# Pointwise steps and sums over K on 32x32 pieces of the array, the second sums moved ahead of V's step, VectorE's order changed, the first copy of Q moved

## The chip, the core and the metric

The kernel runs on one core of one Trainium2 chip. The metric is device time in microseconds (us), the median of several executions. TensorE (PE; its weight loads are PEld) multiplies, VectorE (DVE) and ScalarE (ACT) work on tiles, GpSimd (POOL) does small powers and gathers rows, and SyncE (SP) issues most transfers. Each engine has its own instruction queue and they meet at semaphores.

## What is computed

One layer over 6250 tokens of 256 channels: graph attention, a linear attention in hyperbolic form, and a feed-forward part with a router that picks 2 of 8 experts. The change touches the linear attention alone. Cut to that (the sequence has length one here, so each convolution is a product or a scale):

```python
h = conv1d(logmap0(proj(x)), w_qkv)             # 256 -> 768 channels
t = relu(batchnorm(h))                          # then expmap0, proj, logmap0
s = conv1d(t, w_dw, groups=768)                 # a scale per channel
s = conv1d(s, w_pw, groups=24)                  # 24 blocks of 32x32
q, k, v = split(concat([t, s]))                 # 16 groups of 3 * 32 channels
q, k = relu(q), relu(k)
vk = einsum('ngdl,ngel->ngde', v, k)            # l = 1: v times the sum over k
out = einsum('ngde,ngdl->ngdl', vk, q)
out = out / (sum(v, -1) + 1e-15)
ft = conv1d(out, w_res) + b_res                 # 512 -> 256 channels
```

With one position per sequence, `out` is q times the sum over a group's 32 values of k, where v is not zero. A group of 32 channels takes 32 partitions, so both the pointwise step `w_pw` and the sum over k (a product with a block matrix of ones, `bo`) are 32x32 blocks along the diagonal.

## The kernel before

Tokens lie in 25 blocks (`NB`) of 250 (`BT`), each block of two tiles (`TB`) of 125. Channels lie on partitions, in six chunks of 128: Q in chunks 0 and 1, K in 2 and 3, V in 4 and 5. "T" is the half of the attention that works on `t`, "S" the half that works on the pointwise result `s`.

The program has three stretches. Up to about 204 us the input is scaled and turned, the graph tables are written, and the 256 to 768 product (L1215) is made for all blocks with its batch statistics. From about 204 to 450 us a loop runs over the blocks; the change is there. After that come the router and the two experts.

The loop is one list of steps for each engine, written out by hand, each step with its lag in blocks: in step s a stage with lag 2 works on block s - 2. `steps(NB, [...])` runs each list. Each engine goes through its list strictly in order, and a stage begins with the waits that it needs.

- TensorE: `pointwise_kq` (lag 0; the pointwise step of Q and K), `turn_norms` (1), `res` (2; the product with `w_res`, L1335), `pointwise_v` (0; the pointwise step of V, and with it the sums over K for T), `k_sums_s` (0; the sums over K for S), `turn_xn` (4; L1349), `norms` (0; sums of squares, L1313 and L1316). In the first step `k_sums_s` stands ahead of `pointwise_v`.
- ScalarE: `tanh` (3), `square_s` of K, `keep_k`, `square_s` of Q, `keep_q` (all 0), the ReLU of V of the next block (L931), `square_o` (1; L998), `square_s` of V (0; L959), `square_u` (2; L1007), `more_relu` (steps 1 to 4 only: five blocks' Q), `keep_xn` (4; L1032), `keep_norms` (0; L1027), `square_t` of the next block (L983).
- VectorE: `make_x1` (3), `check_t` (0), `divide_where_needed` (1), statistics of x1 (3), `make_u` (2; L1976 and L1983), `attend_s` (0; L1901), `check_s` (0), `attend_t` (0; L1893 and L1896), `make_xn` (3), `keep_turned` (0), a piece of the graph part (`late_now`).

`divide_where_needed` reads a flag. Where it is set, a long branch divides by sum(v) + 1e-15; otherwise the branch is jumped. In both cases it then raises `fixed`, for which `pointwise_v` of the next block waits. The branch is taken once in this run.

## Time and profile before

| | us |
|---|---|
| median of 3 runs | 791.08 |
| lowest, highest | 790.62, 791.55 |
| profiled execution | 792.75 |
| span of its instructions | 790.7 |
| TensorE busy | 744.1 (94%) |
| VectorE busy | 590.1 (75%) |
| ScalarE busy | 500.8 (63%) |
| GpSimd busy | 509.9 (64%) |

A busy engine is one with an instruction in work; matmuls overlap, and their ends are modelled. The profiled execution is 1.67 us over the median, and 2.05 us of it lie outside the span.

### The profile page before, as it was taken

Reading aid. Unit: us, or ns where it says so; the run is one execution under the profiler, and the core shown is the slowest. Engines: PE = TensorE matmul, PEld = TensorE weight load, DVE = VectorE, ACT = ScalarE, POOL = GpSimd, SP = SyncE. Lnnn points to the kernel's source line nnn.
Section 4 is the critical chain, followed back from the end, with each engine's and each line's share of the span. In section 5 each row is a group of like instructions: output and inputs, shape, how many; then the busy total and the mean of one; then the engine's idle time right before and its main releaser. Section 6 shows DMA issues by size and latency. Waiting matters only on the chain.

```text
span 790.7 us, 16845 instructions
## 1 busy us (share of the span) xinstructions
PE 744.1 (94%) x5512; PEld 624.8 (79%) x5512; DVE 590.1 (75%) x1693; ACT 500.8 (63%) x1163; POOL 509.9 (64%) x693
## 2 busy tenths in 40 slices
PE   5899999999899999999929989999999999999995
PEld 4678888888666666666626677999999999999994
DVE  6873478888769898888997865766776777677675
ACT  2567344989889888888828616555555555555640
POOL 3430678777457888888826742576677766768654
PEclk9999999999999999999968999999999999999999
DMA  9855122222102211111110113000000000000001
GB/s 213 219 155 159 44 54 53 61 49 60 30 19 63 61 54 45 52 35 55 32 43 25 38 33 102 4 24 28 14 27 23 18 27 21 21 27 15 27 27 40
DMA packets 35430, 41.43 MB, mean 52 GB/s; under 512 B 11520, under 2 KB 20696, under 8 KB 35339
## 3 DMA queue, kind: packets, MB, share of 16 engines
q1 hardware_dynamic: 22355, 30.71, 13.4%
q0 software_dynamic: 8000, 6.82, 4.0%
q10 hardware_dynamic: 4984, 2.79, 1.5%
q8 instruction: 45, 0.74, 0.4%
q14 instruction: 46, 0.38, 0.2%
HBM read 25.59 MB, written 14.60 MB: 51 GB/s over the span
## 4 chain that ended last, share of the span: by engine, by line
PE 74%; DVE 6%; POOL 6%; issue 5%; ACT 5%; DMA 2%; SPq 0%; POOLq 0%; DVEq 0%; ACTq 0%
PE ps L1465 18%; PE ps L1504 17%; PE ps L1335 10%; PE ps L1225 7%; PE ps L1215 6%; PE ps L1313 5%; PE ps L1194 4%; ACT Z L931 3%; POOL asrc L622 2%; PE ps L1519 2%; PE ps L1349 2%; PE ps L1323 2%; POOL L L619 1%; ACT Z L927 1%; PE ps L1182 1%
## 5 line engine op out<-in xcount | busy, mean ns | idle before, releaser
L1215 PE MATMUL ps<-Z,L 128*128 128x250 f32 x600 | 126.9, 373 | 0.0
L1215 PEld LDWEIGHTS ps<-Z,L 128*128 128x128 f32 x600 | 113.6, 189 | 13.2
L1086 ACT ACTIVATE Z<-Z,b1s 128x250 f32<-128x250 f32 x144 | 70.0, 503 | 71.7 <-DVE Z L2147 71.7
L1335 PE MATMUL ps<-wr,Z 128*125 128x256 f32 x400 | 92.7, 384 | 0.0
L931 ACT ACTIVATE Z<-Z,bn_o,bn_s 128x250 f32<-128x250 f32 x150 | 81.2, 598 | 1.0 <-DVE bn_o L1855 1.0
L1093 ACT ACTIVATE L<-ps 128x250 f32<-128x250 f32 x144 | 54.3, 379 | 42.9 <-PE ps L1465 40.8
L1335 PEld LDWEIGHTS ps<-wr,Z 128*125 128x125 f32 x400 | 73.1, 188 | 10.2 <-issue 0.4
L2147 DVE TENSOR_TENSOR Z<-ps,L 128x250 f32<-128x250 f32 x144 | 59.4, 415 | 19.5 <-PE ps L1465 17.2
L1225 PE MATMUL ps<-Z,pw 64*64 64x250 f32 x600 | 55.5, 389 | 16.8 <-issue 15.1
L619 POOL DMA_INDIRECT L<-xt_table,idst x36 | 44.2, 1228 | 40.5 <-issue 39.3
L1736 DVE BATCH_NORM_STATS2 L<-Z 128x6 f32<-128x250 f32 x140 | 49.2, 407 | 26.3 <-ACT Z L927 26.2
L927 ACT ACTIVATE Z<-ps 128x500 f32<-128x500 f32 x75 | 43.4, 579 | 30.9 <-PE ps L1215 29.5
L771 POOL TENSOR_TENSOR L<-Z 128x500 f32<-128x500 f32 x23 | 31.5, 1368 | 46.0 <-ACT Z L1086 46.0
L622 POOL DMA_INDIRECT asrc<-xt_table,isrc x40 | 48.6, 1215 | 12.2 <-issue 12.2
L1465 PE MATMUL ps<-Z 128*128 128x250 f32 x192 | 56.3, 374 | 0.0
L1225 PEld LDWEIGHTS ps<-Z,pw 64*64 64x64 f32 x600 | 26.2, 134 | 37.8 <-issue 25.1
L1194 PE MATMUL ps<-L,Z 128*125 128x264 f32 x200 | 50.5, 398 | 0.9 <-ACT Z L883 0.9
L1313 PE MATMUL ps<-L,ones 128*32 128x250 f32 x600 | 49.0, 387 | 1.1 <-issue 0.8
L1504 PEld LDWEIGHTS ps<-Z 128*125 128x125 f32 x368 | 47.2, 187 | 2.0
L1504 PEld LDWEIGHTS ps<-L 128*125 128x125 f32 x368 | 47.1, 187 | 2.0
L1504 PE MATMUL ps<-Z 128*125 128x128 f32 x368 | 47.7, 272 | 0.0
L1504 PE MATMUL ps<-L 128*125 128x128 f32 x368 | 47.5, 272 | 0.0
(274 smaller groups left out, 2000.0 us busy)
## 6 DMA issues: line engine op xcount, KB each, us to landing
Z<-in_x SPq DMA_DIRECT2D x25, 250.0 KB
out<-L SPq DMA_DIRECT2D x24, 250.0 KB
xt_table<-L SPq DMA_DIRECT2D x25, 231.0 KB
Z<-in_x SPq DMA_DIRECT2D x1, 2016.0 KB
g_table<-gg SPq DMA_DIRECT2D x25, 62.5 KB
gg<-g_table SPq DMA_DIRECT2D x25, 62.5 KB
Z<-in_x SPq DMA_DIRECT2D x1, 1344.0 KB
Z<-in_w SPq DMA_DIRECT2D x2, 512.0 KB, 3.7
```

Source lines behind the costliest of these rows:

```text
L622: g.indirect_dma_start(left_at[:, t, :], None, xt_table, bass.IndirectOffsetOnAxis(ap=isrc[0:TP, j:j + 1].bitcast(U32), axis=0), element_o ...
L931: a_.activation(zc(b, c), zc(b, c), ACT.Relu, bias=bn_o[:, c:c + 1], scale=bn_s[:, c:c + 1]).then_inc(done.sem, 1)
L1086: a_.activation(to, of, ACT.Gelu, bias=b1s[:, f // NF, f % NF:f % NF + 1]).then_inc(gelu_done, 1)
L1093: a_.activation(kp[:, s, k - 1], ps[:, bank, 0:BT], ACT.Copy).then_inc(product_kept[s].sem, 1)
L1194: last = mm(ps[0:TP, 2 + 2 * (b % 2) + t, 0:XT], h_raw(b, k)[:, t * TP:(t + 1) * TP], wg[:, k, :], start=(k == 0), stop=(k == KD - 1))
L1215: last = mm(ps[:, group_bank(n), h * BT:(h + 1) * BT], wq[:, k, c * 128:(c + 1) * 128], h_raw(b, k), start=(k == 0), stop=(k == KD - 1))
L1225: return mm(to[cols_], lhsT[rows_, HALF * a:HALF * a + HALF], rhs[rows_], start=True, stop=True)
L1313: last = mm(ps[32 * q:32 * q + 32, 5, 0:BT], ones[:, 0:32], of, start=(i == 0), stop=(i == 3), skip_group_check=True)
L1335: last = mm(res_bank(b, t), ob(b, c, 1)[:, t * TP:(t + 1) * TP], wr[:, c, :], start=(c == 0), stop=(c == NO - 1))
L1465: mm(ps[:, bank, 0:BT], of, by, start=first, stop=True, skip_group_check=True).then_inc(product[s].sem, 1)
L1504: last = mm(ps[0:TP, bank, 0:HD2], of[:, k], by[:, k], start=(first and k == 0), stop=(k == NF - 1), skip_group_check=True)
L2147: v_.tensor_tensor(to, ps[:, bank, 0:BT], kp[:, s, k - 1], ALU.add).then_inc(product_sum[s].sem, 1)
```

## The change

`quarter` becomes `group`: a product of 32 rows by 32 columns of the array, with row piece i going to column piece i XOR step. The steps are chosen so that the sixteen products of Q and K, and the sixteen of V and the T sums, all use different 32x32 pieces; the eight S sums use eight different ones. Each stage has twice as many matmuls. Results of four row pieces that share a column piece go to four banks, so the banks are laid out anew, and `turn_xn` now uses bank 2, which is also K's first bank. K's channels, their weights and parameters are reordered to match (`K_TURN`), `w_res`'s last chunk is loaded in two halves, and the long branch loses two copies because V's result already lies where it is needed. Core of the diff:

```diff
+        K_TURN = (1, 3)
+        Q_STEP, K_STEP, V_STEP, KST_STEP, KSS_STEP = (0, 2), (1, 3), (0, 2), (1, 3), (0, 2)
+        Q_BANK, K_BANK, SUM_BANK, NORM_BANK, V_BANK, RES_BANK = 0, 2, 3, 4, 5, 7
+        XN_BANK = K_BANK
+        KSS_AT = 260
...
             square_s(0, R_Q)
+            keep_q(0)
             act.wait_ge(bn_done.sem, bn_done.count(2))
...
-                (0, keep_q),
+                (0, later(keep_q)),
...
-            def quarter(to, lhsT, rhs, a, e):
-
-                rows_, cols_ = slice(HALF * a, HALF * a + HALF), slice(HALF * e, HALF * e + HALF)
-                return mm(to[cols_], lhsT[rows_, HALF * a:HALF * a + HALF], rhs[rows_], start=True, stop=True)
+            def group(to, lhsT, rhs, i, step):
+
+                rows_, cols_ = slice(GROUP * i, GROUP * i + GROUP), slice(GROUP * (i ^ step), GROUP * (i ^ step) + GROUP)
+                return mm(to[cols_], lhsT[rows_, GROUP * i:GROUP * i + GROUP], rhs[rows_], start=True, stop=True)
...
-                    pe.wait_ge(att.sem, att.count(b - 1, 1))
+                    pe.wait_ge(att.sem, att.count(b - 1, 2))
+                    if b >= 5:
+                        pe.wait_ge(xn_kept.sem, xn_kept.count(b - 5))
...
-                for h in range(NH):
-                    cq, ck = 2 * R_Q + h, 2 * R_K + h
-                    for a in range(2):
-                        quarter(bank_half(R_Q, h), pw[:, cq, :], zc(b, cq), a, a)
-                        last = quarter(bank_half(R_K, h), pw[:, ck, :], zc(b, ck), a, 1 - a)
+                for i in range(4):
+                    for h in range(NH):
+                        cq, ck = 2 * R_Q + h, 2 * R_K + h
+                        group(bank_half(Q_BANK + h, 0), pw[:, cq, :], zc(b, cq), i, Q_STEP[h])
+                        last = group(bank_half(K_BANK + h, 0), pw[:, ck, :], zc(b, ck), i, K_STEP[h])
...
+                pe.wait_ge(s_sq.sem, s_sq.count(b, 2))
+                pe.wait_ge(k_kept.sem, k_kept.count(b))
+                pe.wait_ge(q_kept.sem, q_kept.count(b))
+                for i in range(4):
+                    for h in range(NH):
+                        cv, ck = 2 * R_V + h, 2 * R_K + h
+                        last_v = group(bank_half(V_BANK + h, 1), pw[:, cv, :], zc(b, cv), i, V_STEP[h])
+                        last_k = group(bank_half(Q_BANK + h, 1), bo, zc(b, ck), i, KST_STEP[h])
...
-                    pe.wait_ge(att.sem, att.count(b - 1))
+                    pe.wait_ge(att.sem, att.count(b - 1, 1))
+                    pe.wait_ge(nrm_kept.sem, nrm_kept.count(b - 1))
...
                     pe.wait_ge(s_sq.sem, s_sq.count(b))
+                    pe.wait_ge(att.sem, att.count(b, 1))
...
-                (0, lambda b: None if b else k_sums_s(b)),
+                (0, k_sums_s),
                 (0, pointwise_v),
-                (0, lambda b: k_sums_s(b) if b else None),
...
             def attend_s(b):
                 dve.wait_ge(q_kept.sem, q_kept.count(b))
+                dve.wait_ge(kst_done.sem, kst_done.count(b))
+                dve.wait_ge(t_sq.sem, t_sq.count(b))
                 dve.wait_ge(kss_done.sem, kss_done.count(b))
```

The two waits on `att` are those of `pointwise_kq` and `k_sums_s`; the third, added one is in `norms`. VectorE's list now begins with `check_t`, then `make_x1`, and has `attend_s`, `make_u`, `attend_t`, `check_s` where it had `make_u`, `attend_s`, `check_s`, `attend_t`. On ScalarE the copies of K's weights (R_K of `wq`) are six instead of four, twice, and `w_res` is loaded by three transfers instead of one. The tail's idle matmuls and the first hidden products change banks.

How this stands on TensorE, one step of the loop from the sixth on, before (L1225 are the quarters, L1323 `turn_norms`, L1335 `res`, L1349 `turn_xn`, L1313 `norms`):

```order
L1225 MATMUL ps<-Z,pw 64x250 [waits q_kept,k_kept,s_sq,att,relu_q,relu_k]
L1225 MATMUL ps<-Z,pw 64x250 x7
L1323 MATMUL ps<-sel,L 125x2 [waits norm_kept]
...
L1335 MATMUL ps<-wr,Z 125x256 [waits u_made,fixed]
L1335 MATMUL ps<-wr,Z 125x256 x7
L1225 MATMUL ps<-Z,pw 64x250 [waits att,fixed,relu_v]
...
L1225 MATMUL ps<-L,bo 64x250 [waits att,k_kept]
L1225 MATMUL ps<-L,bo 64x250 x3
L1349 MATMUL ps<-ident,L 128x125 [waits xn_kept,xn_made]
...
L1313 MATMUL ps<-L,ones 32x250 [waits o_sq,nrm_kept,s_sq,t_sq]
```

And the same step after the change (L1239 are the 32x32 products, L1343 `turn_norms`, L1355 `res`, L1369 `turn_xn`, L1333 `norms`):

```order
L1239 MATMUL ps<-Z,pw 32x250 [waits k_kept,q_kept,att,s_sq,xn_kept,relu_q,relu_k]
L1239 MATMUL ps<-Z,pw 32x250 x15
L1343 MATMUL ps<-sel,L 125x2 [waits norm_kept]
...
L1355 MATMUL ps<-wr,Z 125x256 [waits u_made,fixed]
L1355 MATMUL ps<-wr,Z 125x256 x7
L1239 MATMUL ps<-L,bo 32x250 [waits nrm_kept,att,k_kept]
L1239 MATMUL ps<-L,bo 32x250 x7
L1239 MATMUL ps<-Z,pw 32x250 [waits k_kept,s_sq,q_kept,fixed,relu_v]
...
L1369 MATMUL ps<-ident,L 128x125 [waits xn_kept,xn_made]
...
L1333 MATMUL ps<-L,ones 32x250 [waits o_sq,att,nrm_kept,s_sq,t_sq]
```

The S sums have moved from behind V's step to ahead of it, the first row has gained `xn_kept`, and `norms` has gained `att`.

VectorE in one step of the loop, before, from the statistics of x1 on (L1976 and L1983 are `make_u`, L1901 `attend_s`, L1907 `check_s`, L1893 and L1896 `attend_t`, L2007 `make_xn`):

```order
L2002 BN_AGGR mv<-st 125x2 [waits x1] x2
L1976 SCALAR_TENSOR_TENSOR se<-npw,cc 125x2 [waits u_made,scale_n]
L1983 SCALAR_TENSOR_TENSOR L<-ps,se,brow 125x256 [waits res_done,se_done,xn_turned]
L1983 SCALAR_TENSOR_TENSOR L<-ps,se,brow 125x256 [waits res_done]
L1901 TENSOR_TENSOR Z<-ps,L 128x500 [waits kss_done,q_kept]
L1907 TENSOR_SCALAR L,chk<-L 128x500 [waits checked,s_sq]
L1893 SCALAR_TENSOR_TENSOR L<-Z,ps 128x500 [waits s_sq,t_sq,att,s_done,kst_done]
L1896 TENSOR_TENSOR Z<-L,Z 128x500 [waits att]
```

And after (in the same order of names L1996 and L2003, L1924, L1930, L1914 and L1917):

```order
L2022 BN_AGGR mv<-st 125x2 [waits x1] x2
L1924 TENSOR_TENSOR Z<-ps,L 128x500 [waits t_sq,kss_done,kst_done,q_kept]
L1996 SCALAR_TENSOR_TENSOR se<-npw,cc 125x2 [waits u_made,scale_n]
L2003 SCALAR_TENSOR_TENSOR L<-ps,se,brow 125x256 [waits res_done,se_done,xn_turned]
L2003 SCALAR_TENSOR_TENSOR L<-ps,se,brow 125x256 [waits res_done]
L1914 SCALAR_TENSOR_TENSOR L<-Z,ps 128x500 [waits s_sq,t_sq,att,s_done,kst_done]
L1917 TENSOR_TENSOR Z<-L,Z 128x500 [waits att]
L1930 TENSOR_SCALAR L,chk<-L 128x500 [waits checked,s_sq]
```

`attend_s` now stands ahead of `make_u`.

## Rows read from the trace of the kernel before

**Rows 1.** The page: the chain that ended last, share of the span by engine.

```profile
PE 74%; DVE 6%; POOL 6%; issue 5%; ACT 5%; DMA 2%; SPq 0%; POOLq 0%; DVEq 0%; ACTq 0%
```

**Rows 2.** Windows: a step, the first steps, the branch; us, busy, PEclk, DMA, GB/s.

```profile
213.00:222.00 9.00, 7.38 (x81) 4.84 (x82) 5.12 (x17) 8.32 (x17) 4.68 (x6) 0.81 0.06 8
...
349.44:358.36 8.92, 8.92 (x100) 6.04 (x102) 8.31 (x25) 7.86 (x19) 7.82 (x15) 1.00 0.08 23
...
416.00:419.00 3.00, 3.00 (x28) 1.58 (x31) 2.97 (x7) 1.49 (x8) 1.70 (x4) 0.50 0.00 0
```

**Rows 3.** Timeline, PE, one step: start, length, engine, line, what, count.

```profile
349.31 1.08 PE L1225 MATMUL ps<-Z,pw 64*64 64x250 f32 x16
...
350.31 0.60 PE L1323 MATMUL ps<-sel,L 128*125 128x2 f32 x4
350.77 3.70 PE L1335 MATMUL ps<-wr,Z 128*125 128x256 f32 x16
354.40 0.42 PE L1225 MATMUL ps<-Z,pw 64*64 64x250 f32 x1
...
354.41 0.42 PE L1225 MATMUL ps<-Z,pw 64*64 64x250 f32 x1
...
355.10 0.37 PE L1225 MATMUL ps<-Z,bo 64*64 64x250 f32 x1
...
355.29 0.60 PE L1225 MATMUL ps<-L,bo 64*64 64x250 f32 x8
355.82 0.65 PE L1349 MATMUL ps<-ident,L 125*128 125x125 f32 x4
356.40 0.41 PE L1313 MATMUL ps<-L,ones 128*32 128x250 f32 x3
...
358.23 1.08 PE L1225 MATMUL ps<-Z,pw 64*64 64x250 f32 x16
```

**Rows 4.** Timeline, ACT, the same step: V's square to the next norms.

```profile
355.63 0.59 ACT L959 ACTIVATE L<-ps 128x500 f32<-128x500 f32 x1 [0.58 <-PE ps L1225]
...
356.14 0.42 ACT L1007 ACTIVATE L<-L 125x256 bf16<-125x256 f32 x1
...
357.77 0.20 ACT L1032 ACTIVATION_READ_ACCUMULATOR Z<-ps 128x1 f32 x1
...
358.36 0.38 ACT L1027 ACTIVATE L<-ps 128x250 f32<-128x250 f32 x1 [0.39 <-PE ps L1316]
```

**Rows 5.** Timeline, DVE: the same step, and `make_u` where nothing disturbs it.

```profile
355.63 0.88 DVE L1983 SCALAR_TENSOR_TENSOR L<-ps,se,brow 125x256 f32<-125x256 f32 x2
...
356.42 0.67 DVE L1901 TENSOR_TENSOR Z<-ps,L 128x500 f32<-128x500 f32 x1
...
357.00 0.66 DVE L1907 TENSOR_SCALAR_CACHE_REDUCE L<-L 128x500 bf16<-128x500 f32 x1
...
414.18 0.16 DVE L1976 SCALAR_TENSOR_TENSOR se<-npw,cc 125x2 f32<-125x2 f32 x1
414.44 0.88 DVE L1983 SCALAR_TENSOR_TENSOR L<-ps,se,brow 125x256 f32<-125x256 f32 x2
```

**Rows 6.** Timeline, the first step of the loop: PE, ACT, DVE.

```profile
211.16 1.89 PE L1313 MATMUL ps<-L,ones 128*32 128x250 f32 x24 [0.28 <-ACT L L959]
213.47 1.08 PE L1225 MATMUL ps<-Z,pw 64*64 64x250 f32 x16 [0.42 <-DVE Z L1901]
...
212.02 0.59 ACT L969 ACTIVATE L<-ps 128x500 f32<-128x500 f32 x1 [1.00 <-DVE gg L1775]
...
212.64 0.68 DVE L1901 TENSOR_TENSOR Z<-ps,L 128x500 f32<-128x500 f32 x1
```

**Rows 7.** Timeline, end of the long branch: DVE, PE.

```profile
410.84 0.29 DVE L1963 COPY L<-L 64x250 f32<-64x250 f32 x1
...
413.07 0.65 PE L1225 MATMUL ps<-Z,pw 64*64 64x250 f32 x1 [13.98 <-issue]
```

More of the change, by code:

```diff
@@ L204, in gps_layer @@
         sqs = take(NC * BT).rearrange("p (r n) -> p r n", r=3)
+        sqr = take(NH * BT)
+        skr = take(NH * BT)
         sqo = take(NO * BT)
-        skr = take(NH * BT)
-        sqr = take(NH * BT)
         US = 3
@@ L429, in gps_layer @@
         KINDS = (R_K, R_Q, R_V)
+        K_TURN = (1, 3)
[3 more added lines that the diff above has]
+        KSS_AT = 260
+        assert all(KST_STEP[h] == K_TURN[h] and KSS_STEP[h] == K_TURN[h] ^ K_STEP[h] ^ Q_STEP[h] for h in range(NH))
         EARLY_RELU, EARLY_Q, RELU_AT = 30, 20, (1, 1, 2, 3, 4)
@@ L440, in gps_layer, with s_of @@
         S_KQ, S_V = 1, 2
-        HALF = 64
+        def s_of(r):
+            first = {R_Q: Q_BANK, R_K: K_BANK, R_V: V_BANK}[r]
+            return ps[:, first:first + NH, BT:2 * BT] if r == R_V else ps[:, first:first + NH, 0:BT]
         def edge_step(i):
@@ L873, in later_load @@
                 if n == 14:
-                    act.dma_start(wr[:, :, :], w_res.rearrange("(k p) d -> p k d", p=128)).then_inc(late_in, 16)
+                    wr_v = w_res.rearrange("(k p) d -> p k d", p=128)
+                    act.dma_start(wr[:, 0:NO - 1, :], wr_v[:, 0:NO - 1]).then_inc(late_in, 16)
+                    for e in range(2):
+                        act.dma_start(wr[64 * e:64 * e + 64, NO - 1, :], wr_v[64 - 64 * e:128 - 64 * e, NO - 1]).then_inc(late_in, 16)
                 if n == 15:
@@ L1262, in pointwise_v @@
                     pe.wait_ge(fixed.sem, fixed.count(b - 1))
-                    pe.wait_ge(att.sem, att.count(b - 1, 2))
                 else:
-                    pe.wait_ge(z_kept.sem, 3 * NB - 3)
-                for h in range(NH):
-                    cv, ck = 2 * R_V + h, 2 * R_K + h
-                    for a in range(2):
-                        last_v = quarter(bank_half(4 - h, 1), pw[:, cv, :], zc(b, cv), a, a ^ h)
-                        last_k = quarter(bank_half(3 + h, 0), bo, zc(b, ck), a, 1 - (a ^ h))
+                    pe.wait_ge(z_kept.sem, 3 * NB - 1)
+                pe.wait_ge(s_sq.sem, s_sq.count(b, 2))
[6 more added lines that the diff above has]
+                        last_k = group(bank_half(Q_BANK + h, 1), bo, zc(b, ck), i, KST_STEP[h])
                 last_v.then_inc(s_done.sem, 1)
@@ L1281, in k_sums_s @@
                 if b:
-                    pe.wait_ge(att.sem, att.count(b - 1))
+                    pe.wait_ge(att.sem, att.count(b - 1, 1))
+                    pe.wait_ge(nrm_kept.sem, nrm_kept.count(b - 1))
                 else:
                     pe.wait_ge(z_kept.sem, 3 * NB)
-                for a in range(2):
-                    last_0 = quarter(bank_half(1, 0), bo, skr[:, 0:BT], a, a)
-                    last_1 = quarter(bank_half(2, 0), bo, skr[:, BT:2 * BT], a, 1 - a)
+                for i in range(4):
+                    last_0 = group(ps[:, SUM_BANK, KSS_AT:KSS_AT + BT], bo, skr[:, 0:BT], i, KSS_STEP[0])
+                    last_1 = group(ps[:, NORM_BANK, KSS_AT:KSS_AT + BT], bo, skr[:, BT:2 * BT], i, KSS_STEP[1])
                 last_0.then_inc(kss_done.sem, 1)
@@ L1306, in norms @@
                     if b == NB:
-                        last = mm(ps[32 * i:32 * i + 32, 5, 0:BT], ones[:, 0:32], sqo[:, i * BT:(i + 1) * BT], start=True,
+                        last = mm(ps[32 * i:32 * i + 32, NORM_BANK, 0:BT], ones[:, 0:32], sqo[:, i * BT:(i + 1) * BT], start=True,
                                   stop=True, skip_group_check=True)
@@ L1322, in turn_norms @@
                 for t in range(TB):
-                    last = mm(ps[0:TP, 5, 256 + 2 * t:258 + 2 * t], nsb[:, t * TP:(t + 1) * TP], (sel if b < NB else sel_o)[:], start=True,
+                    last = mm(ps[0:TP, NORM_BANK, 256 + 2 * t:258 + 2 * t], nsb[:, t * TP:(t + 1) * TP], (sel if b < NB else sel_o)[:], start=True,
                               stop=True, skip_group_check=True)
@@ L1420, in hidden_0 @@
                     for k in range(KD):
-                        last = mm(ps[:, f % 4, 0:BT], w1s[:, f // NF, k, (f % NF) * 128:(f % NF + 1) * 128],
+                        last = mm(ps[:, 4 + f % 4, 0:BT], w1s[:, f // NF, k, (f % NF) * 128:(f % NF + 1) * 128],
                                   h_of(0, k), start=(k == 0), stop=(k == KD - 1))
@@ L1452, in times @@
                         pe.wait_ge(product_sum[1 - s].sem, product_sum[1 - s].count((g - 1) // 2, SUM_12))
+                if n == P2 and g == 1:
+                    pe.wait_ge(w_dve, 1)
                 if n == P2 and g < 2:
@@ L1717, in _ @@
                     for h in range(NH):
-                        p = q ^ 2 if r == R_K and h == 0 else q
+                        p = q ^ K_TURN[h] if r == R_K else q
                         v_.tensor_copy(per3[32 * p:32 * p + 32, :, 2 * r + h],
@@ L2024, in _ @@
             steps(NB, [
+                (0, lambda b: check_t(b) if b != 1 else None),
                 (3, make_x1),
-                (0, lambda b: check_t(b) if b != 1 else None),
                 (1, divide_where_needed),
@@ L2030, in _ @@
                 (3, moments_of_x1),
+                (0, attend_s),
                 (2, make_u),
-                (0, attend_s),
+                (0, attend_t),
                 (0, check_s),
-                (0, attend_t),
                 (3, make_xn),
```

88 lines of the change are left out of this document (41 added, 47 removed).

## The prediction

> **What bounds the kernel now.** I read the page first: three quarters of the chain that ended last is TensorE [rows 1]. The windows then show one step of the loop that the change touches: of 8.92 us TensorE is busy for all 8.92 at full clock, while VectorE is busy 8.31 and ScalarE 7.86 [rows 2]. So TensorE's own sequence sets the step. The timeline gives its pieces, from the start of one to the start of the next [rows 3]: Q and K's step 1.00, turned norms 0.46, `res` 3.63, V's step with the T sums 0.89, S sums 0.53, turned xn 0.58, norms 1.83; sum 8.92. The second thing to see is how near the other engines are. ScalarE ends its copy of the turned xn at 357.97 and then idles 0.39 us before it takes the norms [rows 4]; V's square ends at 356.22, and the norms begin at 356.40 [rows 3, 4]. The bound is TensorE's, with under half a microsecond of slack on ScalarE.
>
> **The array on 32x32 pieces.** Q and K's step is 8 products, two for each quarter, each product two records: four rounds on a quarter. Later rounds follow at about 0.21 us: V's first starts at 354.40 and its last, in the fourth round, at 355.10 [rows 3]. In each round four records start within about 0.02 us. On sixteen pieces the same work needs two rounds. If the pieces run side by side, Q and K's step saves two rounds, 0.42, less 0.06 for sixteen starts instead of four: 1.00 becomes 0.64. V's step runs from 354.40 to 355.10 + 0.37 = 355.47, so 1.07; it becomes about 0.24 + 0.08 + 0.37 = 0.69. The S sums have one product a piece before and after: two rounds, 0.44, to the next start.
> No row shows more than four pieces at once. The bounds are these: 0.36 gained in each of the two steps, or nothing gained where only eight pieces run together, or a loss. I take the gain, as the starts of four are 0.01 us apart, and sixteen such starts fit in one round.
> The pieces of one bank are worth a look: V's two row halves, both into bank 4, start at 354.40 and 354.41 [rows 3]. [...]
>
> **What is late next.** TensorE's sequence alone would fall to 0.64 + 0.46 + 3.63 + 0.44 (S sums) = 5.17 up to the start of V's step, and then to the norms. These wait for V's square: 0.69 for V's step, 0.16 from its end to ScalarE (355.47 to 355.63), 0.59, and about 0.12 back: 1.56. They now also wait for `attend_s`: 0.69 + 0.16 + 0.67 + 0.12 = 1.64 [rows 3 to 5]. With norms at 1.83 the next Q and K would start 3.47 after V's step, a step of 8.64, 0.28 less than now.
> But the change adds a wait to that start: Q and K's step of block b waits for the copy of the turned xn of block b - 5, since both use bank 2. ScalarE makes that copy late in the step before, behind `square_u`, which waits for `make_u`. And `make_u` now stands behind `attend_s` on VectorE, which can't start before V's step has ended. Before, `make_u` started at 355.63, by itself, and `attend_s` came behind it [rows 5]. Followed from the start of V's step:
> V's step 0.69; to VectorE 0.16 (as for ScalarE); `attend_s` 0.58 to the next start (356.42 to 357.00); `se` 0.26 (414.18 to 414.44); first half of `make_u` 0.44 (half of 0.88) [rows 5]; to ScalarE 0.10, my estimate from the gaps above; both squares and both copies 1.83 (356.14 to 357.97) [rows 4]; to TensorE 0.12. Sum 4.18, against 3.47.
> The step is then 5.17 + 4.18 = **9.35 us, 0.43 more** than 8.92. TensorE stands still for 0.7 us in each. VectorE waits for V's step in place of working, so its earlier `check_t` gives nothing: it has only to be ready when V's step ends, some 6 us after the norms' copy. The 0.36 + 0.38 saved on the array go into this wait.
>
> **The sum.** This wait holds for blocks 5 to 24: 20 steps, one of them with the long branch, so 19 x 0.43 = 8.2. In steps 2 to 4 the wait is not there yet, but the turned norms wait for ScalarE's copy of the norms, which stands behind the same squares and, in these steps, behind extra ReLUs; I take the same 0.43 for each, 1.3, and between nothing and 0.8 as its bounds. Together +9.5.
> The first step: the norms start at 211.16 and now need `attend_s`, which VectorE reaches only at 212.64 and ends at 213.32; the next Q and K start at 213.47 [rows 6]. Norms would start at 213.4 and end 1.9 later. That is +1.9 less about 0.4 for shorter steps: +1.5. The earlier copy of Q takes away ScalarE's wait of 1.00 at 212.02, but VectorE is busy until its own row at 212.64, so it hides nothing on the path. The wider gap may cost clock, which is 0.81 on average in these steps already [rows 2]: up to 1 more.
> The long branch: VectorE drops two copies, the first shown, 0.3 each [rows 7], and joins two products: -0.7. [...] Together -2.0.
> Extra weight copies and transfers on ScalarE lie in the first stretch, beside TensorE's product; four small copies are under 1 us, at nothing as ScalarE waits for TensorE there; 1 us if that cover is gone. Changed banks in the tail: nothing.
> 9.5 + 1.5 - 2.0 = +9.0. The profiled execution has 792.75, 1.67 over the median of 791.08, so 801.75 there and **800.1** at the median, for which I write 800.
>
> **The rivals.**
> A. The pieces don't run more than eight at a time. Then Q and K's step and V's stay as long as they are: +0.42 each, both in the chain above, so 22 steps x 0.84 = 18.5 on top: 818.6. For it: no row has over four. Against: four starts cost next to nothing.
> B. Faster. The chain over `make_u` does not bind, and TensorE's 8.64 does. That needs the chain 0.7 us shorter than summed, below 3.47 from V's start; then 19 x -0.28 = -5.3, nothing in steps 2 to 4, and 1.5 and -2.0 as above, -5.8 in all: 785.3. For it: the latencies between engines (0.16 twice, 0.10, 0.12) are read off or estimated to a few hundredths only, and the end of V's step is a modelled one. Against: the other links are rows of work on engines whose order is fixed, 3.1 us of the 4.18.
> [...]
> D. Both even out: the chain is shorter by half of those 0.7 us, 789.5 to 792.7.
>
> **How the numbers follow.** Forecast 0.55, with its own range 795 to 806 (0.15 a step either way, start and branch 1.5). A 0.11, C 0.02, B 0.22, D 0.10. A difference under 0.2% can't be told from none here. Slower 0.55 + 0.11 + 0.02 = 0.68, same 0.10, faster 0.22. From 785 to 820 the range leaves out C, the upper part of A and about a third of B, 0.12 in all.
>
> **What would show it.** In the steady loop the distance from one copy of norms to the next: 9.35 for the forecast, 8.64 for B, about 10.2 for A. Q and K's step should show idle time ahead of it, some 0.7 us, ended by the copy of the turned xn on ScalarE, and ScalarE should idle about 0.9 us ahead of `square_u`, ended by `make_u`. Sixteen records of Q and K should start within 0.1 us; if they come in groups of four or eight, 0.2 apart, it is A. In the first step the norms should start near 213.4. The prediction is wrong if TensorE stays busy through the step.

## The result, and the profile after

| | before | after |
|---|---|---|
| median, us | 791.32 (4 runs, 790.62 to 793.94) | 811.59 (4 runs, 810.65 to 820.14) |
| ratio to before, 95% interval | | 1.0265 (1.0238 to 1.0293) |
| span of the profiled execution | 790.7 | 808.9 |
| TensorE busy | 744.1 | 737.2 |

The change makes the kernel 20.3 us slower. The forecast was 800.0, in a range from 785 to 820: the sign and the main wait were right, and the size came out at over twice the +9 of the sum. TensorE has 7 us less work and the span is 18.2 us longer. (The two profiled executions are 18 us apart and not 20.3, as the one of the changed kernel, 810.65, was its shortest.)

The chain of waits on the page now names TensorE for less (it answers to [rows 1]), but it adds up to 42% only, so it was followed back through less than half of the span and says nothing of the loop:

```profile
PE 38%; DVE 1%; issue 1%; POOL 1%; ACT 1%; DMA 0%; POOLq 0%; SPq 0%; DVEq 0%; ACTq 0%
```

Everything happens in the loop. ScalarE's copy of the norms starts once in a block, and marks the steps; the last one starts at 453.55 before and at 471.55 after. The table takes the 18.0 us apart by these marks.

| stretch (copy to copy) | before | after | more | forecast |
|---|---|---|---|---|
| start, to the first copy | 213.47 | 217.24 | 3.8 | 1.5, with step 1 |
| step 1 | 9.34 | 10.33 | 1.0 | |
| steps 2 to 4 | 27.51 | 28.81 | 1.3 | 1.3 |
| step 5 | 8.48 | 11.20 | 2.7 | 0.4 |
| 15 steps, 6 to 20 | 135.26 | 144.74 | 9.5 | 6.5 |
| the step with the long branch | 25.94 | 24.26 | -1.7 | -2.0 |
| the last ones | 33.55 | 34.97 | 1.4 | 1.3 |

One steady step, TensorE on the timeline of the changed kernel (it answers to [rows 3]; L1239 are the 32x32 products, L1343 the turned norms, L1355 `res`, L1369 `turn_xn`, L1333 norms):

```profile
364.58 0.72 PE L1239 MATMUL ps<-Z,pw 32*32 32x250 f32 x32 [0.54 <-ACT Z L1045]
365.23 0.60 PE L1343 MATMUL ps<-sel,L 128*125 128x2 f32 x4
365.68 3.70 PE L1355 MATMUL ps<-wr,Z 128*125 128x256 f32 x16
369.31 0.61 PE L1239 MATMUL ps<-L,bo 32*32 32x250 f32 x10
369.56 0.39 PE L1239 MATMUL ps<-Z,bo 32*32 32x250 f32 x1
...
369.76 0.40 PE L1239 MATMUL ps<-Z,pw 32*32 32x250 f32 x5
...
370.31 0.37 PE L1239 MATMUL ps<-Z,bo 32*32 32x250 f32 x1
370.61 0.65 PE L1369 MATMUL ps<-ident,L 125*128 125x125 f32 x4
371.67 0.41 PE L1333 MATMUL ps<-L,ones 128*32 128x250 f32 x3 [0.42 <-ACT L L976]
...
374.19 0.72 PE L1239 MATMUL ps<-Z,pw 32*32 32x250 f32 x32 [0.62 <-ACT Z L1045]
```

The brackets are what was forecast: Q and K's step stands idle for 0.62 us until ScalarE has copied the turned xn (L1045). ScalarE in the same step, from V's square on (it answers to [rows 4]):

```profile
370.77 0.59 ACT L976 ACTIVATE L<-ps 128x500 f32<-128x500 f32 x1 [0.36 <-PE ps L1239]
372.22 0.42 ACT L1020 ACTIVATE L<-L 125x256 bf16<-125x256 f32 x1 [0.86 <-DVE L L2003]
...
373.85 0.20 ACT L1045 ACTIVATION_READ_ACCUMULATOR Z<-ps 128x1 f32 x1
373.94 0.38 ACT L1040 ACTIVATE L<-ps 128x250 f32<-128x250 f32 x1
```

`square_u` (L1020) waits 0.86 us for `make_u`, and the norms' copy at the end no longer waits for anything. VectorE, which it waited for (it answers to [rows 5]; L1924 is `attend_s`, L1996 and L2003 are `make_u`):

```profile
370.78 0.68 DVE L1924 TENSOR_TENSOR Z<-ps,L 128x500 f32<-128x500 f32 x1 [0.15 <-PE ps L1239]
371.37 0.24 DVE L1996 SCALAR_TENSOR_TENSOR se<-npw,cc 125x2 f32<-125x2 f32 x1
371.70 0.88 DVE L2003 SCALAR_TENSOR_TENSOR L<-ps,se,brow 125x256 f32<-125x256 f32 x2
```

The start on TensorE's timeline (it answers to [rows 6]; L1181 is idle work), then step 5:

```profile
213.65 3.54 PE L1333 MATMUL ps<-L,ones 128*32 128x250 f32 x24 [2.13 <-DVE Z L1924]
217.12 0.70 PE L1239 MATMUL ps<-Z,pw 32*32 32x250 f32 x32
...
219.95 0.69 PE L1239 MATMUL ps<-L,bo 32*32 32x250 f32 x16 [1.61 <-ACT L L987]
220.57 2.50 PE L1181 MATMUL ps<-ident,ones 128*128 128x128 f32 x10
...
256.62 0.72 PE L1239 MATMUL ps<-Z,pw 32*32 32x250 f32 x32 [1.61 <-ACT Z L1045]
...
257.73 5.38 PE L1355 MATMUL ps<-wr,Z 128*125 128x256 f32 x16
```

The first norms start at 213.65, where they were forecast (213.4), but take 3.54 instead of 1.89: the clock granted in them is 0.52, where it was 1.00 before. In step 5 `res` takes 5.38 instead of 3.70, behind a wait of 1.61, at a granted clock of 0.68. The windows give the clock (length, busy us and count of PE, PEld, DVE, ACT, POOL, then PEclk; they answer to [rows 2]):

```profile
204.00:217.24 13.24, 9.08 (x142) 4.87 (x155) 9.67 (x27) 7.67 (x17) 3.08 (x3) 0.87 0.11 24
...
256.38:267.58 11.20, 10.26 (x136) 7.10 (x136) 6.89 (x22) 7.92 (x21) 7.18 (x13) 0.85 0.16 42
267.58:277.27 9.69, 8.58 (x136) 5.96 (x136) 8.08 (x22) 7.94 (x21) 7.93 (x15) 1.00 0.22 64
```

### The profile page after: what moved, and what is told of

Its sections match the earlier page's. It is cut to its first block and busy times, and to the rows that moved or that the text cites. A ratio compares the mean times of both kernels' runs of the same rounds, so it can differ in the third digit from the quotient of the medians.

```text
span 808.9 us, 18898 instructions
## 1 busy us (share of the span) xinstructions
PE 737.2 (91%) x6512; PEld 621.7 (77%) x6512; DVE 583.9 (72%) x1690; ACT 501.3 (62%) x1167; POOL 518.6 (64%) x693
## 5 line engine op out<-in xcount | busy, mean ns | idle before, releaser
L1355 PE MATMUL ps<-wr,Z 128*125 128x256 f32 x400 | 94.4, 389 | 0.0
L1355 PEld LDWEIGHTS ps<-wr,Z 128*125 128x125 f32 x400 | 74.3, 191 | 10.7 <-issue 0.4
L2167 DVE TENSOR_TENSOR Z<-ps,L 128x250 f32<-128x250 f32 x144 | 59.7, 416 | 20.4 <-PE ps L1486 18.1
L1239 PE MATMUL ps<-Z,pw 32*32 32x250 f32 x1200 | 40.0, 384 | 26.6 <-issue 13.6
L1333 PE MATMUL ps<-L,ones 128*32 128x250 f32 x600 | 49.7, 390 | 14.7 <-ACT L L976 11.4
L976 ACT ACTIVATE L<-ps 128x500 f32<-128x500 f32 x75 | 44.5, 593 | 13.9 <-PE ps L1239 13.7
L1333 PEld LDWEIGHTS ps<-L,ones 128*32 128x32 f32 x600 | 27.6, 113 | 30.6 <-issue 22.8
L1239 PEld LDWEIGHTS ps<-Z,pw 32*32 32x32 f32 x1200 | 18.1, 104 | 40.7 <-issue 38.5
```

The lines of the kernel that those rows point to most:

```text
L1239: return mm(to[cols_], lhsT[rows_, GROUP * i:GROUP * i + GROUP], rhs[rows_], start=True, stop=True)
L1333: last = mm(ps[32 * q:32 * q + 32, NORM_BANK, 0:BT], ones[:, 0:32], of, start=(i == 0), stop=(i == 3), skip_group_check=True)
L1355: last = mm(res_bank(b, t), ob(b, c, 1)[:, t * TP:(t + 1) * TP], wr[:, c, :], start=(c == 0), stop=(c == NO - 1))
L2167: v_.tensor_tensor(to, ps[:, bank, 0:BT], kp[:, s, k - 1], ALU.add).then_inc(product_sum[s].sem, 1)
```

## The experiments

The first theory was the prediction's: the wait of Q and K's step for the xn copies carries the step. Rivals: another wait of the new order, the start, or the clock. All ratios are to the kernel before, run on the same chip in the same job; its median lay between 791.3 and 793.7 there, so medians of different jobs compare to about 2 us.

**1. Does the xn copy carry the step?** `xn_first`: the changed kernel, ScalarE's list:

```diff
+                (4, keep_xn),
                 (2, square_u),
                 (0, more_relu),
-                (4, keep_xn),
```

> The changed kernel with one thing moved: on ScalarE the copy of the turned xn (keep_xn) stands ahead of square_u and more_relu. Theory W (the wait of Q and K's step for that copy, behind make_u and square_u, sets the step): the copy falls into ScalarE's idle time ahead of square_u, Q and K's step starts when the norms end, the step falls from 9.5 to 9.6 us to about 8.95 (start of Q and K to start of the norms 7.09, norms 1.83), and the slow step at 256 us goes with its wait: 19 x 0.6 + 2 = 13 us less, about 798. Rival P (the 32x32 products themselves, their issue or their number, cost the time): the order on ScalarE changes nothing beyond 2 us, about 811.

Measured 805.95 (1.0166, 1.0139 to 1.0192), commonest step 9.25. The wait of Q and K's step was gone, but the step stopped at 9.25. The profiled execution was its fastest (799.57). What was late now, on TensorE's timeline, then GpSimd's flag, then ScalarE (L1011 is `square_o`, L976 V's square):

```profile
360.46 0.65 PE L1239 MATMUL ps<-L,bo 32*32 32x250 f32 x16
361.29 0.37 PE L1239 MATMUL ps<-Z,pw 32*32 32x250 f32 x1 [0.17 <-issue]
...
363.38 0.41 PE L1333 MATMUL ps<-L,ones 128*32 128x250 f32 x3 [0.81 <-ACT L L976]
```

```profile
359.85 0.37 POOL L683 CROSS_LANE_REDUCE flag<-chk 128x1 f32<-128x4 f32 x1
```

```profile
361.22 1.04 ACT L1011 ACTIVATE L<-Z 128x1000 f32<-128x1000 f32 x1 [0.62 <-DVEq L1989]
362.25 0.59 ACT L976 ACTIVATE L<-ps 128x500 f32<-128x500 f32 x1
```

V's step no longer follows the S sums directly: it waits for `fixed`, which the divide raises once it has read GpSimd's flag. It starts 1.07 us after the end of the flag (360.22 to 361.29), and 1.06 to 1.09 after it in each of the 17 steps between 247 and 398 us. `square_o` waits for `fixed` as well, V's square stands behind it on ScalarE, and the norms wait for V's square. A second loop had been hidden behind the first.

`u_first` (the changed kernel, `make_u` ahead of `attend_s` again):

> The changed kernel with make_u ahead of attend_s on VectorE, as it was before. Theory W: make_u no longer waits for V's step, so square_u and the xn copy come earlier; but in the steps in which VectorE is late (the graph part's product) attend_s is pushed behind and the norms wait for it: step 8.9 to 9.3 us, 4 to 12 us less than 811.6. Rival P: no change beyond 2 us.

Measured 812.35 (1.0245, 1.0201 to 1.0289): nothing won. From 300 to 400 us the wait of Q and K's step is gone, but TensorE idles 10.4 us ahead of the norms in 10 steps, where the changed kernel has 4.7. Undoing VectorE's order inside the new wiring moves the wait and does not remove it.

**2. The parts put on the kernel before.** `b_wait` adds `pe.wait_ge(xn_kept.sem, xn_kept.count(b - 5))` to Q and K's step of the kernel before; `b_order` puts its `attend_s` ahead of `make_u`; `b_both` does both.

> The kernel before with the wait of Q and K's step for the xn copy of block b - 5, and nothing else. Theory W: the copy ended 0.26 us ahead of that step in the trace (357.97 against 358.23), so the wait is free: 791 to 792. Rival: the wait alone costs 0.3 us a step, 797.

> The kernel before with attend_s ahead of make_u on VectorE, and nothing else. Theory W: make_u comes some 0.8 us later, ScalarE's 0.39 us of slack ahead of the norms' copy is used up, but Q and K's step there doesn't wait for ScalarE and covers the rest: 791 to 793. Rival O (this order alone costs the time): 799 or more.

> The kernel before with both: attend_s ahead of make_u, and the wait for the xn copy. Theory W: each is free alone, together they close the loop V's step, sums, attend_s, make_u, squares, xn copy, Q and K's step. There, from V's step to the end of the S sums 1.50, then 0.15, 0.58, 0.26, 0.44, 0.10, 1.83, 0.12 = 4.98, and 5.09 back to V's step: 10.1 us a step against 8.92, 19 x 1.15 = 22 us more, about 813. Rival: they don't add up, below 797.

Measured: `b_wait` 795.18 (1.0020, 0.9999 to 1.0040); `b_order` **811.86** (1.0244, 1.0211 to 1.0278); `b_both` 821.53 (1.0357, 1.0340 to 1.0375). The wait alone costs nothing that can be told from none. The order alone, which I had taken for free, costs nearly as much as the whole change (814.26 in this job, see 3). `b_both` has steps of 10.15, where 10.1 was summed; the changed kernel, with the same order and wait, is 7.3 us under it, and that is what the rest of the change gives back. VectorE in `b_order` shows `make_x1` (L1991) waiting for GpSimd's scale, and in the same kernel ScalarE's `square_o` (L998) waits for the divide (L1969), which V's step needs too:

```profile
284.37 0.88 DVE L1991 SCALAR_TENSOR_TENSOR Z<-L,sg,Z 125x256 f32<-125x256 f32 x2 [1.03 <-POOL sg L713]
...
287.42 0.68 DVE L1901 TENSOR_TENSOR Z<-ps,L 128x500 f32<-128x500 f32 x1 [0.48 <-PE ps L1225]
```

```profile
285.69 1.04 ACT L998 ACTIVATE L<-Z 128x1000 f32<-128x1000 f32 x1 [0.31 <-DVEq L1969]
286.99 0.59 ACT L959 ACTIVATE L<-ps 128x500 f32<-128x500 f32 x1 [0.26 <-PE ps L1225]
```

**3. The same kernel again, the start and the clock.** `after_again` is the changed kernel. `start_early` does `attend_s(0)` between the two halves of the last edge sums on VectorE. `clock_5` puts 8 idle matmuls ahead of Q and K's step of block 5.

> The changed kernel once more, beside the others: 810 to 813.

> The changed kernel with attend_s of block 0 pulled into the middle of VectorE's last graph sums, so that the first norms need not wait for their end. Theory: the first norms start near 211.6 instead of 213.65 and run at full clock (1.9 instead of 3.5 us), the graph sums end 0.6 later: 3 to 5 us less than 811.6. Rival: the flag of block 0 or the last graph sums become the late ones and nothing is gained, within 1 us.

> The changed kernel with 8 idle matmuls ahead of Q and K's step of block 5, in its first long wait (1.61 us). Theory: only the clock is at stake there: res of the next step takes 3.70 instead of 5.38 us, 1.5 to 2 us less than 811.6, nothing else. Rival (the step at 256 us is long for another reason): no change, or 0.3 more.

Measured 814.26 (1.0257, 1.0234 to 1.0279), 812.79 (1.0240, 1.0211 to 1.0269) and 812.38 (1.0239, 1.0222 to 1.0256). `start_early` had its first copy at 214.76 instead of 217.24, and lost the 2.5 in step 2 (11.86 instead of 9.36), where the clock fell in the norms behind an idle 1.95 (0.76 granted from 222.30 to 224.30) and `res` took 5.36 (0.68). `clock_5` took step 5 from 11.20 to 9.81 (granted clock 1.00 from 252 to 268 us, `res` 3.70) and its loop ended 0.6 sooner, not 1.4, as the step with the long branch took 25.09 instead of 24.26 there. Step 5 was 11.20 in `after_again` and `start_early` too: this fall of the clock belongs to the kernel. The one at the first norms does not: in `after_again` they took 1.89, at a granted clock of 1.00, behind an idle 2.25, and the clock fell later: the idle work at 222.77 took 2.50 at 0.50. From the first Q and K step of the loop to the second copy of the norms it is 18.7 before, 23.4 in the changed kernel and 21.3 in `after_again`. Neither term is large enough for the missing 11 us.

One more thing is in `b_order`. GpSimd's power in `scale_of_u` (L704), in the view of that one line: first the kernel before, then `b_order`.

```profile
L704 POOL TENSOR_TENSOR sg<-sg,nhalf x25: 713/714/716, 231.1 to 458.9; 125x2 f32<-125x2 f32 x25
```

```profile
L704 POOL TENSOR_TENSOR sg<-sg,nhalf x25: 713/1332/1342, 231.8 to 477.3; 125x2 f32<-125x2 f32 x25
```

The numbers are shortest, median and longest in ns. The same power takes 0.62 us longer in most blocks of `b_order`, and it stands in the loop that the next runs are about. This part of the cost is `b_order`'s own: in the changed kernel, whose VectorE runs `check_s` at that moment (L1930, for instance from 364.18, the power from 364.43), the median is 0.79.

**4. What the second loop is.** Theory L: V's step, `attend_s`, `make_u`, `square_u`, GpSimd's scale, a gather, its last scale, `make_x1`, the divide, V's step of the next block. The divide needs GpSimd's flag alone, so I put it ahead of `make_x1`: `xn_div` on top of `xn_first`, `b_order_div` on top of `b_order`.

```diff
                 (0, lambda b: check_t(b) if b != 1 else None),
+                (1, divide_where_needed),
                 (3, make_x1),
-                (1, divide_where_needed),
```

`xn_pool` and `xn_div_pool` have the gather ahead of `rstd_of_x1` and `scale_of_u` on GpSimd.

> The changed kernel with the xn copies ahead of the squares of u on ScalarE, and VectorE's divide_where_needed (which opens V's step of the next block) ahead of make_x1 instead of behind it. Theory L (a loop through GpSimd: V's step, attend_s, make_u, square_u, scale_of_u, gather, last scale, make_x1, divide, V's step of the next block): with the xn copies first the loop's late link was V's step waiting for the divide behind make_x1; the divide needs only GpSimd's flag, so it now runs about 1 us sooner, V's step stands behind the S sums again, and the step falls from 9.25 to about 9.0 to 9.1: 26 steps by .2 are 5 us, so 799 to 802. Theory T (the TensorE order itself bounds: S sums to V's end 1.37, norms, QK): the step stays at 9.2 to 9.3 and the time at 805 to 808. Rival: make_x1 waits now behind the divide's flag read, and the time does not fall or grows.

> The kernel before with attend_s ahead of make_u on VectorE (811.9 alone, steps about 9.8), and in addition divide_where_needed ahead of make_x1. Theory L: most of what the order cost came through V's step waiting for the divide behind make_x1 (V's step waited for it in the trace); with it gone the step falls from 9.8 to about 9.1 to 9.3 (the wait of the turned norms for the norms copy stays), so 796 to 802. If the norms copy's wait, behind square_u on ScalarE, were the whole cost, the time stays at 808 to 812.

> The changed kernel with the xn copies first on ScalarE, and on GpSimd the gather of a late block's rows ahead of rstd_of_x1 and scale_of_u instead of between scale_of_u and the last scale. Theory L: the gather (1.1 us on GpSimd) stands in the loop in the first part of the steps, in those where a gather is left to issue, and its place takes about .2 to .5 off the steps there: 800 to 804. Where the loop runs through the wait for tanh and not through the gather, nothing changes: 805 to 807.

> Both moves on top of the xn copies first: the divide ahead of make_x1 and the gather ahead of rstd_of_x1. Theory L: with the divide moved, make_x1 and with it the gather no longer stand in V's loop, so this one equals the one with the divide alone within 1 us (799 to 802). If both links were still late one behind the other, it would be 2 to 4 us below it.

Measured 820.46 (1.0355), 820.41 (1.0328), 807.26 (1.0191) and 810.55 (1.0209). None came out as theory L had it: the first two went the other way, by 14.5 and 8.6 us over the kernels they were built on, `xn_pool` did nothing, since the last scale then waited for ScalarE, and `xn_div_pool` came 9.9 us under `xn_div`, where the two were to be equal. GpSimd in `xn_div` shows why (L715 to L719 the scale, L661 the gather, L724 and L726 the last scale, L683 the flag):

```profile
357.55 0.26 POOL L719 TENSOR_TENSOR sg<-sg 125x2 f32<-125x2 f32 x1
358.00 1.35 POOL L661 DMA_INDIRECT asrc<-xt_table,isrc  x1 [0.19 <-issue]
359.43 0.23 POOL L724 TENSOR_SCALAR sg<-sg 125x2 f32<-125x2 f32 x1
359.74 0.20 POOL L726 TENSOR_TENSOR sg<-sg 125x2 f32<-125x2 f32 x1
359.93 0.37 POOL L683 CROSS_LANE_REDUCE flag<-chk 128x1 f32<-128x4 f32 x1
```

VectorE behind it, in the same kernel:

```profile
361.43 0.88 DVE L2011 SCALAR_TENSOR_TENSOR Z<-L,sg,Z 125x256 f32<-125x256 f32 x2 [2.09 <-issue]
...
363.33 0.68 DVE L1924 TENSOR_TENSOR Z<-ps,L 128x500 f32<-128x500 f32 x1
```

The flag is queued on GpSimd behind the gather and the last scale. It ends at 360.30, and the divide lets the rest go about 1.1 us later. With the divide first, `make_x1` and its statistics are held as well, and `attend_s` comes at 363.33. The loop's link is the flag's place in GpSimd's queue; that was the wrong step of theory L. So theory L2: the same loop through the flag. `flag` swaps two lines of GpSimd's list (on top of `xn_first`), `flag_div` has the divide ahead of `make_x1` as well, `flag_div_pool` the gather ahead too, and `b_order_flag` is `b_order_div` with the swap.

```diff
+                (1, raise_flag),
                 (3, last_scale_of_u),
-                (1, raise_flag),
...
+                (2, lambda b: gather_piece(b) if b >= 2 else None),
                 (3, rstd_of_x1),
                 (2, scale_of_u),
-                (2, lambda b: gather_piece(b) if b >= 2 else None),
```

> The changed kernel with the xn copies first and raise_flag ahead of the last scale on GpSimd, VectorE's order left as it is (make_x1 ahead of the divide). The divide still stands behind make_x1, which waits for the last scale, .37 later than before. Theory L2: the loop goes by make_x1 and gains nothing or loses .2 a step: 805 to 812. If the flag alone carried it: 798 to 802.

> The same without the gather's move. The flag still stands behind scale_of_u and the gather in the steps that have one, but ahead of the last scale: .6 to .7 us sooner than with the divide alone. Theory L2: steps of about 9.1 to 9.2 instead of 9.8, 799 to 806; worse than with the gather moved by up to 4. Theory T: 805 to 808.

> The changed kernel with the xn copies first on ScalarE, the divide ahead of make_x1 on VectorE, and on GpSimd raise_flag (which the divide waits for) ahead of last_scale_of_u, and the gather ahead of rstd_of_x1. In the run with the divide moved alone the flag was taken at 359.93, directly behind the last scale, and the divide ended at 361.3: the flag, queued on GpSimd behind the gather and the last scale, carried the loop. Theory L2 (the loop V's step, attend_s, make_u, square_u, scale_of_u, gather, last scale, flag, divide, V's step of the next block): the flag can now be taken at about 358.1, the divide ends at about 359.5, 1.4 us ahead of the S sums, make_x1 and its sums no longer hold attend_s, and the norms start about 1 us sooner: steps of 8.9 to 9.0, loop end near 456, 795 to 800. Theory T (TensorE's order alone): steps stay at 9.25, 805 to 808.

> The kernel before with attend_s ahead of make_u (811.9 alone; 820.4 with the divide ahead of make_x1), and in addition raise_flag ahead of the last scale. Theory L2: 820.4 was the flag behind the last scale and the gather; with it ahead of the last scale the steps fall from 10.15 to about 9.5, so 802 to 808. If the norms copy behind square_u on ScalarE carries the cost, it stays at 810 to 820.

Measured 802.89 (1.0146, 1.0111 to 1.0181), 805.96 (1.0192, 1.0151 to 1.0232), **798.06** (1.0072, 1.0047 to 1.0097) and 807.32 (1.0189, 1.0156 to 1.0222). Of the kernels run, only the one with all three moves lets the loop go: the step falls to 8.91, V's step starts 2.1 to 2.6 us behind the flag, and with the same divide order the two moves on GpSimd are worth 22.4 us (820.46 to 798.06; 20.4 where each is taken against the kernel before of its job). The flag alone is 12.5 of them (810.55 to 798.06). The two moves on GpSimd with the divide left behind `make_x1` were not run, so that the divide's own move is needed is not shown; `flag_div` is no faster than `flag`. `flag` fell between its two cases: V's step there starts about 1.7 behind the flag, with `make_x1` in between. `b_order_flag` fell by 13.1 and kept steps of 9.5 to 9.8, with the gather still ahead of its flag and the turned norms waiting for ScalarE. One steady step of `flag_div_pool` on TensorE:

```profile
344.97 0.61 PE L1239 MATMUL ps<-L,bo 32*32 32x250 f32 x10
...
346.27 0.65 PE L1369 MATMUL ps<-ident,L 125*128 125x125 f32 x4
347.33 0.41 PE L1333 MATMUL ps<-L,ones 128*32 128x250 f32 x3 [0.41 <-ACT L L976]
...
349.16 0.71 PE L1239 MATMUL ps<-Z,pw 32*32 32x250 f32 x32
...
353.88 0.61 PE L1239 MATMUL ps<-L,bo 32*32 32x250 f32 x10
```

From S sums to S sums 353.88 - 344.97 = 8.91: 2.36 to the norms, 1.83 of norms, 4.72 to the next S sums. Q and K's step waits for nothing. The last wait is that of the norms for V's square, 0.41.

**5. The start, on the kernel without the loop.** `start_no_idle` is `flag_div_pool` with `attend_s(0)` and `attend_t(0)` inside the last edge sums. `start_idle` has in addition 8 idle matmuls ahead of the S sums of block 1, 5 ahead of its norms, and 3 instead of 5 ahead of its V step.

> The kernel with the loop through GpSimd taken out (xn copies first, flag and gather ahead, divide ahead of make_x1: 798.1, steady steps of 8.91), and in addition attend_s(0) and attend_t(0) inside the last edge sums, 8 idle matmuls ahead of the S sums of block 1 and 5 ahead of the norms of block 1 (instead of 5 behind the S sums of block 1, of which 3 stay). Theory: its loop ended 7.4 us later than before's, of which 8.7 in the first step (3.4 of that the projection of this one profiled execution, the rest the wait of the first norms for attend_s(0), 2.1 to 2.4, and half clock, 1.65, and step 1), 1.4 in steps 2 to 4, against 1.3 won at the long branch. The start placed sooner gives back 2.5 and the held clock 1.5 to 2: loop end near 453 to 456, 792 to 795, level with the kernel before. If the clock falls again in step 2 or 5 as it did with the start alone (812.8 against 811.6): 796 to 799.

> The same with the idle matmuls as they were. Theory: what the idle work is for is the clock alone; without it the start wins 2.5 in the first step and loses 1 to 2.5 again in step 1 to 5 at a lower granted clock: 795 to 798, 2 to 3 above the kernel with the idle work. If the clock is no part of the loss both are equal within 1 us.

Measured 793.27 (12 runs; 1.0017, 1.0000 to 1.0034) and 794.45 (7 runs; 1.0041, 1.0027 to 1.0055). Both have the whole change in them, and the better one is within 0.4% of the kernel before; no version of mine beat it. In the profiled executions the loop ends at 453.48 and 452.71, where it ended at 453.55 before. With the start placed sooner the median is 3.6 us lower (798.06 to 794.45), but the intervals of the two ratios overlap, so how much of it is the start is open; on the changed kernel the same kind of move won nothing (`start_early`). The extra idle work may win 1 more or nothing, as the intervals overlap. It was meant to hold the clock, but the windows of `start_no_idle` show no fall without it:

```profile
204.00:216.00 12.00, 8.99 (x164) 5.33 (x162) 9.32 (x26) 9.43 (x19) 3.27 (x4) 1.00 0.10 25
216.00:226.00 10.00, 6.39 (x130) 4.17 (x131) 5.58 (x21) 8.72 (x17) 4.77 (x7) 1.00 0.07 11
```

Its first norms, on TensorE's timeline, with an idle of 0.80 ahead of them where the changed kernel has 2.13:

```profile
212.78 1.89 PE L1333 MATMUL ps<-L,ones 128*32 128x250 f32 x24 [0.80 <-DVE Z L1926]
```

## Why the prediction was right, and where not

The wait that was forecast is there, and the kernel still lost over twice what the sum gave. Three steps of the prediction failed, each a term of its sum. In the steady steps V's step was given 0.69 from a start 0.44 behind the S sums, as if the S sums left its pieces free: the two take 1.37 together, not 1.13, and with 0.07 more for `se` the 15 steps have 3.0 us over the forecast. In step 5 the same wait was put at 0.7 and no clock with it: it was 1.61, and `res` behind it took 1.68 more, 2.3 us over the forecast in all. At the start the clock was left out of the sum: 3.3 us. The second loop, through GpSimd's flag, is a fourth thing that the prediction did not have; it adds little to this time, but it kept the cure of the first loop from working.

**The array's pieces: right.** Q and K's step is 0.65 to the next start (forecast 0.64), and thirty-two records last 0.72 together. At the end of the long branch, where the granted clock is 0.50, sixteen records of V's step start between 431.53 and 431.64, within 0.11, and the second sixteen only at 431.91 (`pw` are V's products, `bo` those of the T sums, by turns):

```profile
431.53 0.59 PE L1239 MATMUL ps<-Z,pw 32*32 32x250 f32 x1 [13.57 <-issue]
431.53 0.62 PE L1239 MATMUL ps<-Z,bo 32*32 32x250 f32 x1
...
431.64 0.62 PE L1239 MATMUL ps<-Z,bo 32*32 32x250 f32 x1
431.91 0.62 PE L1239 MATMUL ps<-Z,pw 32*32 32x250 f32 x1
```

So rival A is out. Each of V's two banks is written by four row pieces among these sixteen, each to its own partitions, and no record shows one of them waiting for another.

**The chain through `make_u`: right link by link, with two terms too small.** From the S sums (369.31) to the next Q and K (374.19) it takes 4.88 where the forecast had 0.44 + 4.18 = 4.62; the 4.73 ahead of it is exact (364.58 to 369.31). S sums and V's step take 1.37 to the end of V's step, not 0.44 + 0.69 = 1.13: I gave V's step its 0.69 from a start 0.44 behind the S sums, but the S sums and V's products work on the same pieces. The T sums, on pieces that the S sums leave free, start at 369.56, V's products at 369.76, and the last products of the step at 370.31. `se` takes 0.33 instead of 0.26. `attend_s` comes 0.06 sooner than summed, and the rest is within 0.02. That makes 9.61 for this step instead of 9.35; the 15 steps from 6 on have 9.65 on average, against 9.02 before, so 0.63 each instead of 0.43, which is the 3.0 us over the 15 steps.

**The floor of 8.64, and so rival B: wrong by the same term.** `flag_div_pool` has neither wait and still takes 8.91. Add the 0.24 to 8.64, and 0.03 remain. With all waits off the path the pieces gain nothing in a steady step: 8.91 against 8.92. What the array gives back goes into the path S sums, V's step, V's square, norms. So B's 785.3 could not happen. D needed the chain through `make_u` shorter than summed, and it was 0.26 longer. No run has the 32x32 pieces with the S sums behind V's step, where they were before, so what the pieces alone would give is not measured.

**Steps 2 to 4 and the long branch: the numbers right, the first partly by luck.** Steps 2 to 4 have 1.3 for 1.3, but not by the wait that was named: between 226 and 256 us TensorE waits 0.5 for ScalarE's copy of the norms, and 2.5 ahead of the norms for V's square and `attend_s`. The long branch has -1.7 for -2.0; as its step took 24.50 in `after_again` and 25.24 in `b_wait` (24.26 and 25.94 in the two kernels' own traces), that is good to some 0.7. Of the -2.0, 0.7 was VectorE's; no run shows the other 1.3, the products saved at the low clock, by itself. In its place the traces show this: behind the branch the granted clock is 0.50 in both kernels (413.07 to 415.50 before, 431.53 to 434.00 after), the rounds of V's step start about 0.41 apart, against 0.21 at full clock, and from V's first product it takes 1.08 to the turned xn (431.53 to 432.61), where it took 2.71 with the S sums in between (413.07 to 415.78).

**The start: place right, size wrong.** Forecast +1.5 and up to 1 for the clock; measured 4.8 with step 1. The clock was the term too small: the norms took 1.65 more at about half the clock (0.52 granted), and the idle work of step 1 took 2.50 (0.50) where it took 1.65 (1.00) before. How much of it falls here is that execution's chance: counted from the loop's first Q and K step, the start and step 1 have 4.7 more than before in this trace and 2.6 more in `after_again`. The S sums of block 1, now ahead of this idle work, wait 1.61 for ScalarE's copy of K with TensorE idle.

**Step 5: not foreseen.** It is the first in which Q and K's step waits for the xn copy, and there for 1.61, not 0.7, as the extra ReLUs still stood ahead of that copy on ScalarE in step 4; `res` then runs at a granted clock of 0.68, 1.68 longer. Together 2.3 over the forecast. So of 9.0 us that the trace has over the forecast of 9.0, the start has 3.3, step 5 has 2.3 and the steady steps have 3.0.

**"The order alone is free": wrong, and not in the prediction.** It was my expectation for `b_order`. The prediction found one loop through `make_u` and stopped there. The second one, through GpSimd's flag, has a period (the time of one step that it allows) of 9.25 in `xn_first`, under the first one's 9.6, and so left hardly a mark on the sum. It showed as soon as the first was cut. The kernel before has the link too, with little room. Its flag, GpSimd on the timeline:

```profile
352.23 0.78 POOL L670 CROSS_LANE_REDUCE flag<-chk 128x1 f32<-128x4 f32 x1
```

It ends at 353.01, and V's step starts 1.39 us later, at 354.40 [rows 3]. The way from the flag to V's step takes 1.07 where nothing else holds it (experiment 1), so 0.3 us is to spare in this step; in the 17 steps between 244 and 390 us it is between nothing and 1.1. `attend_s` takes 0.58 to the next start ahead of `make_u`, and the slower power adds 0.62. Less the room that is 0.9, and `b_order` shows 0.9 us more in a step (9.8). This is an estimate from one step; no run took the slower power out of `b_order`.

## What to carry to other kernels

When a step of one engine's list is moved behind another's result, follow every consumer of that step around to the point where it started, through all engines' queues, and write down each loop with its period; the longest one sets the time, and curing it brings out the next. A small flag or scale that opens the next block belongs ahead of the slow work in its engine's queue: here moving a 0.37 us reduction and a gather on GpSimd was worth some 20 us with the same order elsewhere. Here a finer cut of the array shortened a stage only as far as the stage ahead of it left the same pieces free (S sums and V's step 1.37 us together, where 1.13 was summed): price two stages on shared pieces together.
